# Denominators directly behind the values, and two turns of the maxima ahead of the values

## What is computed

```
q = relu(layernorm(x)); k = v = relu(ctx)                # 16 heads of 32
att = softmax(q k^T / sqrt(32))                          # 256 x 256 per head
x = x + tanh(g_xattn) * relu((att v) @ ffn_w.T + ffn_b)
y = layernorm(x); y_prev = y shifted by one token
xr = mu_r*y + (1-mu_r)*y_prev;  xk = mu_k*y + (1-mu_k)*y_prev
r = sigmoid(xr @ W_r.T);  ka = square(relu(xk @ W_k.T))
x = x + tanh(g_ffn) * r * (ka @ W_v.T)
```

## Time and profile before

| | before |
|---|---|
| time, median of 3 runs | 2838.47 us (2838.12 to 2844.43) |
| time of the profiled execution | 2841.78 us |
| its span | 2840.0 us |
| TensorE matmuls busy | 2776.0 us, 98% of the span |
| VectorE busy | 2347.4 us, 83% |
| ScalarE busy | 1629.5 us, 57% |
| GpSimd busy | 1047.2 us, 37% |
| granted TensorE clock, mean | 0.995 of full speed |

### The profile page before, as it was taken

The page is one execution under the profiler, slowest core; times in us unless marked ns, Lnnn a source line. Parts: engine busy times, 40 slices in busy tenths (PEclk is TensorE's granted clock), DMA queues, the critical chain, the costliest instruction groups (busy, mean ns, idle before and its releaser), DMA issues.

```text
span 2840.0 us, 70714 instructions
## 1 busy us (share of the span) xinstructions
PE 2776.0 (98%) x22786; PEld 2150.5 (76%) x22786; DVE 2347.4 (83%) x4173; ACT 1629.5 (57%) x2955; POOL 1047.2 (37%) x902
## 2 busy tenths in 40 slices
PE   4899999999999999999999999999999999999998
PEld 2677777777777777777777777777777777777776
DVE  6788888888888888888888888888888888888874
ACT  4556556556556556556556566565565565565552
POOL 0234333333333343343343343343333343433433
PEclk9899999999999999999999999999999999999999
DMA  5544544544544545545545445445445445445431
GB/s 187 151 145 138 160 145 139 156 144 139 161 137 144 158 131 155 149 134 158 147 132 163 144 135 164 144 137 158 147 138 157 143 139 162 135 147 155 133 103 43
DMA packets 407416, 408.82 MB, mean 144 GB/s; under 512 B 165584, under 2 KB 331472, under 8 KB 407376
## 3 DMA queue, kind: packets, MB, share of 16 engines
q1 hardware_dynamic: 355152, 341.18, 41.8%
q10 hardware_dynamic: 52224, 67.12, 6.8%
HBM read 272.90 MB, written 134.22 MB: 143 GB/s over the span
## 4 chain that ended last, share of the span: by engine, by line
PE 96%; DMA 1%; DVE 1%; SPq 1%; issue 0%; ACT 0%; POOL 0%; DVEq 0%; POOLq 0%; ACTq 0%
PE bank L954 51%; PE bank L921 10%; PE bank L935 9%; PE bank L947 9%; PE bank L909 9%; PE bank L879 5%; PE bank L896 3%; PE bank L887 1%; DMA q_st<-m_t 0%; DMA o_dram<-o_val 0%; DVE o_val L721 0%; DVE m_nat L702 0%; DMA k_dram<-k_raw 0%; SPq L252 0%; POOL xr_lo L384 0%
## 5 line engine op out<-in xcount | busy, mean ns | idle before, releaser
L489 ACT ACTIVATE probs<-bank 128x512 f32<-128x512 f32 x1024 | 594.2, 591 | 369.7 <-PE bank L921 369.5
L702 DVE TENSOR_REDUCE m_nat<-bank 128x2 fp32r<-128x512 f32 x1024 | 694.6, 684 | 106.2 <-PE bank L909 106.0
L470 ACT ACTIVATE q_st<-bank 96x512 fp32r<-96x512 f32 x512 | 304.3, 594 | 582.2 <-PE bank L879 581.9
L721 DVE RECIPROCAL o_val<-bank 128x256 f32<-128x256 f32 x256 | 449.3, 1755 | 86.2 <-PE bank L947 44.3
L921 PE MATMUL bank<-q_st,k_st 97*128 97x256 f32 x2048 | 437.4, 295 | 14.0 <-DMA q_st<-m_t 14.0
L909 PE MATMUL bank<-k_st,q_st 96*128 96x256 f32 x2048 | 432.7, 293 | 5.8 <-DVE m_nat L702 4.9
L921 PEld LDWEIGHTS bank<-q_st,k_st 97*128 97x128 f32 x2048 | 346.2, 190 | 80.1 <-issue 26.8
L909 PEld LDWEIGHTS bank<-k_st,q_st 96*128 96x128 f32 x2048 | 358.0, 192 | 57.4 <-DVE m_nat L702 6.4
L391 POOL TENSOR_TENSOR xm<-xm 128x512 f32<-128x512 f32 x128 | 139.9, 1093 | 653.6 <-ACT xm L533 653.6
L358 POOL TENSOR_TENSOR o_lo<-o_mv,o_hi 128x512 fp32r<-128x512 f32 x128 | 164.5, 1285 | 400.9 <-ACT o_hi L496 400.8
L954 PE MATMUL bank<-xk_hi,w_hi 128*128 128x256 f32 x1024 | 299.0, 292 | 0.0
(11 more groups left out here) (88 smaller groups left out, 6057.8 us busy)
## 6 DMA issues: line engine op xcount, KB each, us to landing
k_st<-k_dram SPq DMA_DIRECT2D x256, 256.0 KB, 3.6
k_raw<-ctx_t_dram SPq DMA_DIRECT2D x256, 128.0 KB, 4.2
x_ln<-x_dram SPq DMA_DIRECT2D x256, 128.0 KB
k_dram<-k_high SPq DMA_DIRECT2D x64, 512.0 KB, 3.2
k_dram<-k_raw SPq DMA_DIRECT2D x64, 512.0 KB, 5.8
k_st<-k_dram SPq DMA_DIRECT2D x256, 128.0 KB, 3.5
o_dram<-o_val SPq DMA_DIRECT2D x256, 128.0 KB, 1.7
o_mv<-o_dram SPq DMA_DIRECT2D x512, 64.0 KB, 2.0
```

What stands on the lines that cost most here:

```text
L470: nc.scalar.activation(q_st[0:QK, c, :, P * u:P * u + P], tp_bank[0:QK, :].rearrange("p (g t) -> p g t", g=GR), ACT.Copy).then_inc(q_stack ...
L489: nc.scalar.activation(probs[:, n // GR % 2, n % GR, :, :].rearrange("p v t -> p (v t)"), st_bank[n % 2][:, :], ACT.Exp, scale=SCALE).then ...
L702: nc.vector.tensor_reduce(m_nat[:, c % 2, n % GR, :], s_bank[n % 2][:, :].rearrange("p (u y) -> p u y", u=NU), AX_X, ALU.max, negate=True) ...
L721: nc.vector.reciprocal(o_val[:, :], pv_bank[:, T:2 * T]).then_inc(rden_ready, 1)
```

## The change

TensorE's order alone changes. The denominators of each group come directly behind its values: those of group 3 move ahead of turn(1), those of group 0 stand behind the values with turn(4) now ahead of both, those of group 1 move from step 10 to step 9, ahead of turn(8), and those of group 2 from step 14 to step 13. turn(4), in step 5, and turn(12), in step 13, move from behind the values to ahead of them. The instructions are the same, and so is the order of the turns among each other.

```diff
--- before.py
+++ after.py
@@ -1057,8 +1057,8 @@
                 scores(i, 7)
                 dense(0, 0)
                 values(i - 1, 3)
+                denominators(i - 1, 3)
                 turn(1)
-                denominators(i - 1, 3)
                 dense(0, 1)
 
                 shifted_scores(i, 1)
@@ -1087,8 +1087,8 @@
                 dense(2, 2)
                 scores(i, 12)
                 dense(2, 3)
+                turn(4)
                 values(i, 0)
-                turn(4)
                 denominators(i, 0)
 
                 shifted_scores(i, 6)
@@ -1112,6 +1112,7 @@
                 shifted_scores(i, 9)
                 dense(4, 2)
                 values(i, 1)
+                denominators(i, 1)
                 turn(8)
                 scores(i + 1, 0)
                 dense(4, 3)
@@ -1119,7 +1120,6 @@
 
                 shifted_scores(i, 10)
                 dense(5, 0)
-                denominators(i, 1)
                 turn(10)
                 scores(i + 1, 1)
                 dense(5, 1)
@@ -1137,15 +1137,15 @@
 
                 shifted_scores(i, 13)
                 dense(6, 2)
+                turn(12)
                 values(i, 2)
-                turn(12)
+                denominators(i, 2)
                 scores(i + 1, 4)
                 dense(6, 3)
 
                 shifted_scores(i, 14)
                 dense(7, 0)
                 scores(i + 1, 5)
-                denominators(i, 2)
                 turn(13)
                 dense(7, 1)
```

## The result

| | before | changed |
|---|---|---|
| time, median | 2839.69 us (4 runs) | 2878.61 us (4 runs, 2878.57 to 2881.77) |
| ratio | | 1.0135, 95% interval 1.012 to 1.0149 |
| span of the profiled execution | 2840.0 us | 2876.8 us |
| TensorE matmuls busy | 2776.0 us, 98% | 2740.7 us, 95% |
| batch to batch | 42.98 us | 43.57 us on average, 43.61 in the one below |

The account below looks back on a forecast made before the run. TensorE's own stream was taken as the bound, 42.98 us a batch; its saving of 1.06 is paid back by 1.06 to 1.13 of waiting, +3 us in all: 2841.5 us, range 2831 to 2878.

Parts of the forecast that it names:

- what TensorE saves: TensorE's values-denominators pairs: each takes 1.86 us, and the four groups together save 1.06 us a batch, 68 us in all.
- the turn of step 13 and turn(10): TensorE waits for VectorE's maxima and norm_2: some 0.8 us a batch at step 13's turn, 0.28 at turn(10).
- The hand-over from VectorE: Time from the end of VectorE's operation to the TensorE turn waiting for it, estimated at 0.06 us.
- Behind the late pair: VectorE from head_max 4 on comes 1.73 us later, TensorE 0.30 later; called hidden, by 0.6 us.
- the forecast's own 3: The net slowdown forecast for the whole kernel, +3 us, from a batch 0.07 us longer.
- The first rival: TensorE's saving arrives whole because the turns do not wait: 2770 us; chance 8%.
- The second rival: Seam between values and denominators no cheaper than now: pair costs 2.00 us, +35 us, 2876; chance 8%.
- the third: VectorE's norm_o(3) stays tied to its DMA, head_max 8 and 9 come 1.73 us later: +37 us, 2878; chance 9%.
- The fourth: TensorE's clock falls during waits, 3 us a batch if in each batch: 3020 us; chance 3%.
- The signs: What would show the forecast right, among it TensorE's busy time falling by some 65 us while the span stays.

Follow-up runs that it names:

- e3: The kernel before with the edits of groups 3 and 0 alone (denominators directly behind values, turn(1) behind them, turn(4) ahead); 2811.22 us, ratio 0.989.
- e11: e8 with the last part of stats_1 moved behind copy_m of group 1 and mix_r(i-2) behind head_max(i, 9) and relu_v; 2779.6 us, ratio 0.9789.
- e5: The kernel before with one edit alone, turn(12) ahead of values(i, 2), no denominators moved; 2885.64 us, ratio 1.0158.
- e6: The changed kernel with VectorE's finish(i-2, 0), head_max(i+1, 5) and norm_o(i, 2) ahead of stats_1(i+2); 2856.22 us, ratio 1.0058.
- e7: e6 with turn(12) behind the pair of group 2 instead of ahead of it; 2840.15 us, ratio 1.0004.
- e8: e7 with turn(10) moved behind scores(i+1, 1) and dense(5, 1); 2816.51 us, ratio 0.9913.
- e1: The changed kernel with VectorE's head_max(i+1, 5) and norm_o(i, 2) ahead of finish(i-2, 0); 2886.19 us, ratio 1.0153.

## Why the prediction was wrong

**Right: what TensorE saves.** The pair takes 1.86; e3's two groups saved 0.49 a batch, where 0.50 was forecast; all four saved 1.03 in e11 (41.95 a batch on average, 41.93 the median), where 1.06 was forecast. The denominators' first weight loads start with the last round of the values, at 1464.18 in the pair that starts at 1463.51, and don't wait for these to drain:

```profile
1464.18 0.13 PEld L947 LDWEIGHTS bank<-probs,ones_r 128*32 128x32 f32 x4
```

**Right, but for one term: the turn of step 13 and turn(10).** head_max(i+1, 3) ended at 11.81, as worked out, and e5 shows this wait by itself. turn(10) stood at 4.69 (forecast 4.63), the turn at 11.95 (11.87). The hand-over from VectorE was 0.14 (1463.22 to 1463.36), not the 0.06 estimated; this term was mis-sized and costs 0.08 x 62 = 5 us.

**Wrong: the step "Behind the late pair".** It said that head_max 4 and all behind it on VectorE, norm_o 2 among them, come 1.73 later where TensorE itself is 0.30 later, and called this hidden. But it followed it only to norm_o 3's DMA and to the scores of heads 10 and 11. There it held: TensorE's waits for maxima ahead of scores are 2.6 us in 5 places (4.9 in 4 before). It did not ask who on TensorE waits for norm_o 2, and so put that wait at nothing. That is values(i, 3): line 931 waits for o_ready of the group before, as all values do. norm_o 2 itself was forecast well (on the prediction's own clock it ends at 20.99, 1.80 later than before). TensorE would have been at the values at about 20.68, which is where they start in e6; they started at 21.14 in the batch shown, 21.09 on average. 0.41 x 62 is 25 us. With the 5 above and the forecast's own 3 that makes 33 of the 39 measured. Of the other 6, about 2 are 0.03 a batch that no term covers; where the rest lies is open. e6 shows the wait from the other side: with this wait alone taken away from TensorE, 22 us come back.

**The first rival** (saving arrives whole) did not happen here, since the turns did wait; e11 reached it by other orders.

**The second rival** (no cheaper seam, 2876) and **the third** (norm_o 3 tied to its DMA, 2878) named nearly the measured time and were both wrong in mechanism. The seam is 0.89 from values to denominators and the pair 1.86. VectorE's waits for the DMA of o_val are 2.1 us in one place after the change; before they were 41.6 us over 50 places:

```profile
DVE o_val L721 <- DMA o_dram<-o_val: 41.6, 50, 2.7
```

A time that hits a rival's number does not bear the rival out; its row does.

**The fourth** did not happen: the mean granted clock was 0.994 (0.995 before).

**The signs.** TensorE's busy time fell by 35 us, not by the 65 named. In e11 it falls by 65, to 2711.0, and in e3, where no wait comes in, by 32, which is what e3 saves. So the sign fails where waits come in. I think that the modelled ends of the matmuls ahead of each wait reach into it and count as busy; this is argued, not shown.

## What to carry to other kernels

When a change makes an engine late at one place, list every semaphore that this engine raises behind it, and for each the place that waits, before following the one that seems tight: a bank to be freed is as much a result as a number. A saving in the bounding engine's stream is worth nothing until the other engines' orders follow; here the four pairs went with 39 us lost in one order of turns and VectorE's work, and with 60 us won in another. And look at what runs on GpSimd when moving VectorE's work: in e6 the square started 0.34 us behind the start of the mix's fourth operation (median), in e7 0.02 behind it, and with this shift of 0.3 us operations met that had not met before.

## What the runs showed of the hardware that was not expected

- A VectorE operation of 0.17 us on two numbers per partition took up to 1.27 us beside a GpSimd operation, one of 0.48 up to 1.32, and this hung on which of the two had started first (e8). In the steady state of the kernel before neither was hit; in e8 38 of the 256 operations of line 764 were.
- Such a meeting can cost nothing. In the kernel before, VectorE's operations were longer by 42 us in norm_1 (line 671, 60 operations, 0.54 as a rule and up to 1.36), by 14 us in line 677 and by 4 us in line 745, each beside GpSimd, and yet TensorE's batches in the steady state took 42.98 or 42.99, one like the other. In e8 the 38 us of lines 764 and 665 came ahead of maxima that TensorE needed, and its batches were longer by as much.
- Eight rounds of 32-column matmuls ran at 0.22 from start to start, across the seam between two different stationary operands too (values to denominators 0.89, of which the first round is 0.24). A tail of 0.11 was there only where something of another shape followed.
- The time from the end of a VectorE operation to the start of the TensorE instruction that stood waiting for it hung on the place. It was 0.13 (median) for the turn of the maxima and for turn_xn and 0.15 for the values in the changed kernel, but 0.055 for the scores in e8 (42 times) and for dense(0, 0) in e1 (60 times). Why is open.
